# A pre-norm attention and feed-forward layer: sums of the softmax inverted per half, a tiled end for the last chunk, one block for the general path, and loads moved out of the prologue

## The reference

```python
def attention(x, ...):                       # on layernorm(x)
    qkv = einsum('bse,fe->bsf', x, in_proj_weight) + in_proj_bias
    scores = einsum('bhqd,bhkd->bhqk', q * scale, k)
    blocked = (j <= i) & (j >= i - 16)       # a band just left of the diagonal is blocked
    attn = softmax(where(blocked, -inf, scores))
    ctx = einsum('bhqk,bhkd->bhqd', attn, v)     # heads side by side again
    return einsum('bsf,fe->bse', ctx, out_proj_weight.T) + out_proj_bias
def ffn(x, ...):                             # on layernorm(x), three 256x256 products, no nonlinearity between
    return tanh(x @ weight @ aux_weight1 @ aux_weight2 + bias)
x = x + attention(layernorm(x))
x = x + ffn(layernorm(x))
```

## Time and profile before

| | us |
|---|---|
| time of the kernel, median of 3 runs | 2064.96 (2062.73 to 2069.01) |
| time of the profiled execution | 2062.95 |
| its span, first to last instruction | 2058.0 |
| ACT busy in the span | 1924.7 (94%) |
| PE busy | 1827.9 (89%) |
| DVE busy | 696.1 (34%) |
| POOL busy | 151.5 (7%) |
| first score of stream | at 88.27 |
| end of the last product of probabilities and values | at 1995.29 |
| store of the last chunk issued | at 2043.40 |
| barrier at the end of stream | at 2046.7 |

### The profile page before, as it was taken

One profiled execution on the slowest core, in us unless ns is written; L12 is line 12 of the kernel. 1 busy time (PEld: TensorE's weight loads), 2 busy tenths in 40 slices (PEclk: granted clock), 3 DMA queues, 4 the chain that ended last, 5 costly groups with the idle time before them and its releaser, 6 DMA issues. The chain is left out here.

```text
span 2058.0 us, 100762 instructions
## 1 busy us (share of the span) xinstructions
PE 1827.9 (89%) x47072; PEld 751.1 (36%) x47072; DVE 696.1 (34%) x1366; ACT 1924.7 (94%) x2106; POOL 151.5 (7%) x172
## 2 busy tenths in 40 slices
PE   6599899999999999999999999999998888898872
PEld 3233334343434334343443434343332323232321
DVE  5323332433344343434433343343322112121222
ACT  3499999999999999999999999999999999999970
POOL 1000000101010000101100010000000000000000
PEclk9799999999999999999999999999999999999995
DMA  3400102101230210202231110201111010101010
GB/s 118 137 27 23 58 26 59 36 18 55 58 100 27 58 37 18 64 25 61 57 82 45 30 61 17 60 27 54 54 54 48 13 42 12 47 16 47 8 29 24
DMA packets 93664, 94.39 MB, mean 46 GB/s; under 512 B 17514, under 2 KB 84522, under 8 KB 93234
## 3 DMA queue, kind: packets, MB, share of 16 engines
q1 hardware_dynamic: 93236, 87.84, 14.8%
HBM read 53.09 MB, written 26.25 MB: 39 GB/s over the span
## 5 line engine op out<-in xcount | busy, mean ns | idle before, releaser
L1160 ACT ACTIVATE probs<-scores 128x1024 f32<-128x1024 f32 x2048 | 1886.9, 1113 | 28.6 <-PE scores L1183 26.6
L1202 PE MATMUL outs<-probs,vs 64*32 64x512 f32 x16384 | 1076.5, 590 | 0.2 <-issue 0.2
L1183 PE MATMUL scores<-qs,ks 49*32 49x512 f16 x16384 | 838.6, 383 | 164.1 <-ACT probs L1160 142.9
L1183 PEld LDWEIGHTS scores<-qs,ks 49*32 49x32 f16 x16384 | 233.2, 89 | 1085.4 <-ACT probs L1160 1046.1
L1202 PEld LDWEIGHTS outs<-probs,vs 64*32 64x32 f32 x16384 | 301.2, 106 | 36.7 <-issue 11.3
L871 DVE TENSOR_TENSOR probs<-probs,allowed 128x320 f32<-128x320 f32 (+2 forms) x280 | 149.4, 537 | 308.2 <-ACT probs L1160 307.9
L1241 PE MATMUL spare<-s_xt,w_qkv 64*32 64x256 f32 x3072 | 121.4, 376 | 0.0
L1241 PE MATMUL spare<-w_o,ctx_in 64*32 64x256 f32 x2048 | 80.4, 384 | 21.0 <-DVE ctx_in L896 19.4
L820 POOL TENSOR_TENSOR s_squares<-s_qk_f 128x512 bf16<-128x512 f32 x48 | 61.3, 1278 | 353.0 <-DVE s_qk_f L938 353.0
L814 POOL TENSOR_TENSOR s_x<-s_x,bias_o 128x1024 f32<-128x1024 f32 x16 | 38.1, 2384 | 626.2 <-DMA s_x<-in_x 626.2
L1241 PE MATMUL spare<-w_ffn,s_f_xt 64*32 64x256 f32 x2048 | 81.6, 389 | 3.0 <-DVE s_pre L1043 1.6
(11 more groups left out here) (103 smaller groups left out, 770.5 us busy)
## 6 DMA issues: line engine op xcount, KB each, us to landing
qs<-q_parts SPq DMA_DIRECT2D x192, 64.0 KB
ks<-k_parts SPq DMA_DIRECT2D x192, 64.0 KB
ctx_in<-raw SPq DMA_DIRECT2D x256, 32.0 KB, 2.0
inverse<-row_inverse SPq DMA_DIRECT2D x32, 256.0 KB
s_x<-in_x SPq DMA_DIRECT2D x16, 512.0 KB, 7.2
out<-s_pre SPq DMA_DIRECT2D x16, 512.0 KB, 6.1
s_xin<-in_x SPq DMA_DIRECT2D x12, 512.0 KB, 7.8
q_parts<-s_parts SPq DMA_DIRECT2D x24, 256.0 KB, 2.3
```

Of the source, the lines that this page charges most:

```text
L1160: act.activation(probs[:, u % RING, 2 * slot:2 * slot + 2].rearrange("p c q -> p (c q)"), scores[:, 2 * slot:2 * slot + 2].rearrange("p c ...
L1183: last = pe.matmul(scores[cols, 2 * slot + e], ks[rows, group, keys], qs[rows, group], start=True, stop=True)
L1202: last = pe.matmul(outs[32 * c:32 * c + 32, side], vs[keys, at:at + 2 * HD], probs[keys, u % RING, c], start=(i == 0), stop=(i == KBLOCKS ...
```

## The change

- **Prologue.** SP loads the last chunk's keys and the guards of half 0 alone, and ends. The keys and guards of half 1, w_o, bias_o and bias_f are issued at the start of stream, before the feed-forward weights. Waits for them stand where they are first used (POOL add_bias, PE project_out, DVE add_f_bias of chunk 0).
- **Sums per half.** `move_sums` copies the sums from `raw` straight to the layout 32x64 per four heads, two DMAs per half, ahead of the 8 DMAs of the context. The trip through DRAM (row_sums) is gone. `spread_inverse` writes and spreads the inverses of one half, so half 0 is inverted in slot 40 and scaled in slot 45 of its own step, half 1 in slots 8 and 19 of the next. Per chunk there are 4 + 2 + 2 DMAs for this, before 4 + 1 + 1 + 2.
- **End of the last chunk.** Only half 1 is left to divide. ACT issues its 8 context DMAs. PE works with the whole 128x128 array per tile of 128 tokens, in the four score banks, so DVE adds once and not twice; each tile goes by itself through add, statistics, rsqrt, normalise, transpose, product, bias, tanh, sum and a store of 128 KB. ACT copies the transposed tiles. The range checks stand before the scaling on DVE, and partition_all_reduce before the tiles' rsqrt on POOL.
- **General path.** Its three blocks become one, with one flag test per engine.
- Several semaphores become two counters (dve_step, pool_step), one per engine, that count the same waits.

```diff
@@ first_batch, SP
-            load_chunk(CPB - 1)
+            for par in range(2):
+                sp.wait_ge(parts_out[par], CPB // 2 * 64)
+            load_keys(sp, lay, 0, 0, CPB - 1, k_parts)
+            sp.wait_ge(guard_keys_in, 2 * 16)
             sp.wait_ge(guard_done, 1)
-            for hg in range(HALVES):
-                load_guards(sp, lay, hg, guard)
-            sp.dma_start(keep["w_o"][:], ...).then_inc(rest_in, 16)
-            for dst, src in ((keep["bias_o"], b_o), (keep["bias_f"], b_f)):
-                sp.dma_start(dst[:], src.partition_broadcast(P)).then_inc(rest_in, 16)
-            sp.wait_ge(rest_in, 5 * 16)
+            load_guards(sp, lay, 0, guard)
@@ stream, SP
+            def move_sums(step, hg):
+                done = step * HALVES + hg + 1
+                sp.wait_ge(out_free, done)
+                if step:
+                    sp.wait_ge(inverted, done - HALVES)
+                for side in range(2):
+                    first = (hg * PASS_HEADS + side * HG) * 8
+                    sp.dma_start(sums[first:first + HG * 8], raw[HD:P:32, side]).then_inc(sums_in, 16)
+            def spread_inverse(step, hg):
+                n = step * HALVES + hg
+                sp.wait_ge(inverted, n + 1)
+                heads = row_inverse[hg * PASS_HEADS:(hg + 1) * PASS_HEADS]
+                if step:
+                    sp.wait_ge(inverse_in, (n - 1) * 16)
+                sp.dma_start(heads.rearrange(...), sums_inv[hg * HALF_P:(hg + 1) * HALF_P]).then_inc(inverse_out, 16)
+                sp.wait_ge(inverse_out, (n + 1) * 16)
+                if step:
+                    sp.wait_ge(ctx_scaled, n - 1)
+                sp.dma_start(inverse[:, hg], heads.unsqueeze(1).to_broadcast([PASS_HEADS, HD, CHUNK])
+                             ).then_inc(inverse_in, 16)
@@ run_step, SP
                 move_context(step, 0)
+                spread_inverse(step, 0)
@@ end of stream, SP
-            move_context(NCH - 1, 1)
-            invert_sums(NCH - 1)
-            store_result(NCH - 1)
+            move_sums(NCH - 1, 1)
+            spread_inverse(NCH - 1, 1)
+            for t in range(TPC):
+                sp.wait_ge(result_done, TAIL + t + 1)
+                sp.dma_start(out_tiles[NCH - 1][:, t], pre[:, t]).then_inc(stored, 16)
@@ end of stream, POOL
             add_bias(NCH - 1)
-            f_rsqrt(NCH - 1)
             pool.wait_ge(fine_ready, 3)
             pool.partition_all_reduce(any_bad[:], bad[:], P, bass.bass_isa.ReduceOp.max).then_inc(all_bad, 1)
+            for t in range(TPC):
+                column = slice(t, t + 1)
+                pool.wait_ge(f_stats_done, TAIL + t + 1)
+                pool.tensor_tensor(f_var_eps[:, column], ...).then_inc(pool_step, 1)
+                pool.wait_ge(pool_step, next(pool_steps))
+                pool.tensor_tensor(f_rstd[:, column], ..., ALU.pow).then_inc(f_rstd_done, 1)
@@ run_step, DVE
+                    if r == 40:
+                        invert(step, 0)
+                    if r == 45:
+                        scale_context(step, 0)
                     if finishes:
                         if r == 8:
-                            invert(f)
-                        if r in (19, 20):
-                            scale_context(f, r - 19)
+                            invert(f, 1)
+                        if r == 19:
+                            scale_context(f, 1)
@@ end of stream, ACT
+            for side in range(2):
+                for c in range(HG):
+                    act.dma_start(ctx_in[rows, 1], raw[32 * c:32 * c + HD, side]).then_inc(ctx_moved, 16)
@@ end of stream, PE
+            def tail_out(t):
+                for k in range(HALVES):
+                    last = pe.matmul(scores[:, t, 0:EMB], ctx_in[:, k, t * P:(t + 1) * P], keep["w_o"][:, k],
+                                     start=(k == 0), stop=(k == HALVES - 1))
+                last.then_inc(y_ready, 1)
+            for t in range(TPC):
+                tail_out(t)
+            tail_turn(0)
+            tail_turn(1)
+            tail_project(0)
+            tail_turn(2)
+            tail_project(1)
+            tail_turn(3)
+            tail_project(2)
+            tail_project(3)
@@ general path, each engine (DVE shown)
+            def whole():
+                project.vector(dve)
+                meet(dve, 1)
+                attend.vector(dve)
+                meet(dve, 2)
+                finish.vector(dve)
+            if_bad(dve, keep, whole)
```

366 lines of the change are left out of this document (213 added, 153 removed).

## The result

| | before | after |
|---|---|---|
| median (runs of one comparison) | 2063.85 us (2059.45 to 2069.01, 4 runs) | 2015.94 us (2014.78 to 2018.02, 4 runs) |
| profiled execution | 2062.95 | 2016.49 |
| its span | 2058.0 | 2014.8 |
| first score of stream | 88.27 | 75.20 |
| first score to the last copy of `raw` | 1907.1 | 1908.7 |

The changed kernel takes 0.9767 of the time of before, 95% interval 0.9747 to 0.9786. The forecast was 2025.5 us with a range of 2021.5 to 2035. The four stretches of the table add up to a gain of 43.2 us in the span, where 39.5 was forecast. The rest to the 49.0 us between 2064.96 and 2015.94 lies outside the span and in the choice of the execution that was profiled; both come further down. (Against the 2063.85 of the same comparison the gain is 47.9.)

The account below looks back on a forecast made before the run. ACT's back-to-back exponentials bound the stream and stay; the gain lies outside it: 8.0 (start) + 25.3 (end) + 6.2 (general path) = 39.5 us, taking the median from 2064.96 to 2025.5 us, range 2021.5 to 2035.

Parts of the forecast that it names:

- The start: Prologue: fewer key and guard issues on SP bring the first score to 80.2; gain 8.0 us (6.5 to 8.3).
- the DMA rush: Start: DMA engines 90% busy from 3 to 11 us, read as slowing POOL's 10.3 us configuration load.
- The steady part: Stream: two inversions per chunk and later key loads, taken as 0, between -2 and +1 us.
- The rival of early inversions that stall the stream: Stream: DVE waits in slot 45 for half 0's inverses, costing ACT 3.0 us per step; 2071 us, chance 0.02.
- The end, to the first product: Last chunk: sums first and one half's inverse spread; PE starts the tail at 2005.8, 8.8 us earlier.
- The end, tiles: Tail tile by tile: last store issued at 2018.7 against 2043.40; barrier 25.3 us earlier in total (23 to 27).
- half of that: Tail: two transposes per tile take 0.97 us at half clock, about half of that at full.
- Half clock over the first products: Tail on PE: a tile's product takes 0.89 us at full clock, 1.8 at half; y of tile 0 at 2007.6.
- Whether POOL is ready: End: two POOL configuration loads, around the all-reduce, taken as hidden if each takes under about 6.8 us.
- The rival of the 10.3: End: each POOL configuration takes about 10.3 us, so gain 31.9 and time 2033 us; chance 0.30.
- The general path: After the barrier: one block instead of three, 5.1 us to the end; gain 6.2 us.
- 4.95 more than its span: Whole execution: the profiled one took 2062.95 us against a span of 2058.0; no term changed this.

Follow-up runs that it names:

- e4: The changed kernel with all keys, guards, w_o and biases loaded in the prologue again; 2025.32 us, ratio 0.9802.
- e1: The kernel before with one small POOL addition behind partition_all_reduce; 2064.72 us, ratio 1.0006.
- e2: The changed kernel with partition_all_reduce behind the four rsqrt, as before; 2023.56 us, ratio 0.9793.
- e5: The changed kernel with the last half's 8 context moves issued on SP behind the sums instead of on ACT; 2018.72 us, ratio 0.9778.
- e7: The changed kernel with 23 unused products on PE while it waits for the last scaled context; 2015.57 us, ratio 0.9764.
- e3: The changed kernel with the general path in its three blocks of before; 2024.18 us, ratio 0.9795.
- e11: The changed kernel with the prologue, the computing tail and the three exact blocks of before together; 2052.64 us, ratio 0.9937.
- e12: The changed kernel with old sums through DRAM, old computing tail and three exact blocks; 2051.67 us, ratio 0.994.
- e8: The changed kernel with sums through DRAM, both halves inverted once a chunk, last moves on SP; 2026.90 us, ratio 0.9806.

## Why the prediction was wrong in size

**The start: the step that failed.** The forecast put the first score at 80.2, for "Gain 8.0". It came at 75.20, a gain of 13.1. The 8.0 came out in e4; POOL's part and that of the loads can be told apart to about 1 us only, so the exact match has some luck in it. What is missing is 5.0 us of POOL. Alone they bring the forecast from 2025.5 to 2020.5, below its own range. The prediction used only to price a reload at the end, and never asked why there is a load at 1.3 us at all, though nothing ahead of it in the program calls for one. It is the state that the execution before left, and the change alters that state by its last POOL operation. e1 and e2 show it in both directions. That the DMA rush stretches this load, as the forecast said, fits: 10.3 at the start, 6.04 and 6.88 bare. No run has the load at the start without the rush, so it is not shown.

**The steady part.** Taken as 0 between -2 and +1; it was 1.6 us longer in the two profiled executions. e5 and e7 have 1905.9 and 1907.3 for the same stretch with the same stream, so 1.6 is within what one kernel shows. (The forecast's 1906 for before is a slip: 1995.29 less 88.27 is 1907.0. Nothing in its sum used it.) The rival of early inversions that stall the stream fell: ACT's waits are 4.9 us.

**The end, to the first product.** The forecast had it 8.8 us earlier; it was 8.0. The spread of the inverse landed 4.1 us after its issue and not 3.7, and was issued 0.4 later. The ACT moves took 0.67 each, near SP's 0.6, and were covered; had they stayed on SP the loss was 2.6 (e5).

**The end, tiles.** From first product to last store 12.9 in the forecast, 12.5 measured. From last copy to barrier the gain is 25.5 against 25.3, which is closer than its parts: 0.8 too much for the earlier start, 0.4 too little for the tiles, and 0.6 too little for the store, from whose issue to the barrier it was 3.3 us and is 2.1. One reading was wrong and did no harm: the eight entries of transposes in the earlier trace rows are eight transposes, one entry each, unlike a product's two. Two per tile are then 0.49 at that rate and not 0.97, and the trace has a granted clock of 1.00 there, not half. The "half of that" which the sum took is near the 0.41 to 0.44 of the tail. Half clock over the first products was assumed, and e7 shows it, and what it costs.

**Whether POOL is ready.** Taken as hidden below 6.8 us per load, with the 10.3 of the start as the rival at 0.30. The bare loads took 6.04 and 6.88 us, and the changed kernel's first load began at 1982.1, 7.5 us ahead of the reduce, the second had 8.6 us. So both were hidden. Like is to be set against like: ahead of the reduce a bare load takes 6.04 (e2) and had 7.5, behind it 6.88 (e1) and had 8.6, so 1.4 and 1.7 us were to spare. The larger bare value is at the forecast's bound of 6.8. The figure of about 6 us in the Trainium skill (GPSIMD Engine Reference, section on instruction dispatch) is met by the 6.04; the 6.88 lies 0.9 above it. The rival of the 10.3 fell.

**The general path.** 6.2 forecast, 6.2 measured in the span; e3 has 6.8 for the same step.

**Outside the sum.** The sum was made against one execution, and the step "4.95 more than its span" was carried over unchanged. It became 1.7, which e11 and e12 tie to the old parts in combination; why stays open. The two profiled times are therefore 46.5 apart, 43.2 in the span and 3.3 outside. And the profiled execution of before lies 2.0 under its median, as the forecast said, while that of the changed kernel lies 0.55 over its own: with the narrower scatter the distance between profile and median went too. So 39.5 forecast, 3.7 more in the span (5.1 at the start and 0.2 at the end, less 1.6 in the stream), 3.3 outside it and 2.6 between profile and median make the 49.0. The range was 2021.5 at its lower end because each term's best value was taken and no term stood for what isn't in the diff.

## What to carry to other kernels

If the first instruction of a program waits, ask what state the last one of the execution before left: here the order of two POOL operations at the end moved 5 us at the start. A configuration load is best priced away from a rush of DMAs; and two of them, hidden behind a chain of DMAs that took 10.5 us from last copy to scaling, were free. Where a queue's issues are the path, moving issues behind the first use pays their full price (0.5 us each) until a landing that they had covered becomes the bound.

## What the runs showed of the hardware that was not expected

- POOL's configuration outlives an execution (taking it that the execution before was the same kernel's): first affine_select at 1.57 after an execution that ended with ordinary operations (changed kernel, e1), at 11.63 and 11.66 after one that ended with the reduce (before, e2).
- The time outside the span does not add up from parts: 1.7 us, 2.3 with three blocks, 2.05 with the old tail, 4.0 to 4.8 with both and a third old part. Its cause stays open; ten more semaphores do nothing.
- With the sums moved through DRAM and inverted once a chunk spans scatter by 7.7 to 13.0 us, with sums per half by 5.1 at most, at the same mean DMA load (share 0.16, 44 GB/s from 200 to 1900 us, in e8 and in the changed kernel).
- PE can stand for "issue" in a full stream, up to 2.6 us. Each of the six such waits over 0.4 us that e8 and the changed kernel have in the stream ended 1.4 to 1.6 us after a late 16 KB packet of the trace's instruction queue, with the DMA engines over 90% busy ahead of the packet.
